# A four-chunk, eight-stage network kernel: the softplus of the Mamba stage split into four planner steps, and a new planned order

## The reference, cut to what matters

```python
u = silu(conv(x_part))                       # 512 columns of a chunk, 128 channels on partitions
delta = jax.nn.softplus(einsum('blr,dr->bld', dt, dt_proj_w) + dt_proj_b)
dA  = jnp.exp(delta * A)                     # A = -exp(A_log), 16 states
dBu = delta * Bm * u
h = dA_t * h + dBu_t                         # scan over time, y = sum over states of h * c_t
```

## Time and profile before

| | before |
|---|---|
| median of 3 runs | 1419.3 us (1419.26 to 1420.51) |
| the profiled execution's own time | 1418.26 us |
| its span in the trace | 1416.4 us |
| TensorE (PE) busy | 1322.8 us, 93% |
| PE weight loads (PEld, beside PE) busy | 923.5 us, 65% |
| VectorE (DVE) busy | 1025.9 us, 72%, 3806 instructions |
| ScalarE (ACT) busy | 896.2 us, 63%, with 78 table loads, 100.1 us |
| GpSimd (POOL) busy | 693.5 us, 49% |
| mean granted TensorE clock | 0.96 of full speed |

### The profile page before, as it was taken

How to read it: one execution, slowest core, us unless ns; L and a number is a source line. 1 busy time by engine, 2 the same in 40 slices (tenths; PEclk the granted TensorE clock), 3 DMA queues, 4 the chain that set the end, 5 groups by cost and what they waited for, 6 DMA issues and landing times. The chain is left out here.

```text
span 1416.4 us, 26262 instructions
## 1 busy us (share of the span) xinstructions
PE 1322.8 (93%) x8774; PEld 923.5 (65%) x8774; DVE 1025.9 (72%) x3806; ACT 896.2 (63%) x2487; POOL 693.5 (49%) x699
## 2 busy tenths in 40 slices
PE   9687698889988999999999999999999999998997
PEld 5123365566545787677777677787777888865665
DVE  4998988787689848668688566497798579653253
ACT  6636689786573558776877776546768657643231
POOL 1637255674374535455445547543825424413625
PEclk9659999999998989999999999999999999999999
DMA  7651000100140100110001000301100000043131
GB/s 266 158 133 30 1 1 2 54 2 29 78 127 1 66 1 3 53 63 1 1 2 61 2 31 31 122 1 61 38 42 2 1 1 2 1 150 102 18 90 30
DMA packets 21278, 65.80 MB, mean 46 GB/s; under 512 B 1852, under 2 KB 8252, under 8 KB 18840
## 3 DMA queue, kind: packets, MB, share of 16 engines
q1 hardware_dynamic: 21144, 64.12, 14.1%
HBM read 61.83 MB, written 2.29 MB: 45 GB/s over the span
## 5 line engine op out<-in xcount | busy, mean ns | idle before, releaser
L1360 ACT ACTIVATE arena<-arena 128x256 f32<-128x256 f32 (+3 forms) x792 | 347.5, 443 | 48.0 <-DVE arena L1828 24.0
L1360 ACT ACTIVATE arena<-bank 128x512 f32<-128x512 f32 (+3 forms) x354 | 190.8, 570 | 237.6 <-PE bank L915 158.1
L915 PE MATMUL bank<-XT,W 128*128 128x512 f32 (+1 forms) x752 | 290.1, 524 | 0.6 <-DVE arena L1828 0.6
L2175 POOL TENSOR_TENSOR arena<-arena 128x256 f32<-128x256 f32 x192 | 119.2, 621 | 331.0 <-DVE arena L1843 330.6
L915 PEld LDWEIGHTS bank<-W,arena 128*128 128x128 f32 (+1 forms) x1888 | 232.2, 195 | 54.1 <-issue 38.0
L915 PE MATMUL bank<-W,arena 128*128 128x128 f32 (+2 forms) x1888 | 244.9, 281 | 7.1 <-POOL arena L2148 4.8
L915 PE MATMUL bank<-arena 128*32 128x128 f32 (+8 forms) x2912 | 238.0, 338 | 11.5 <-DVE arena L1849 3.6
L2148 POOL TENSOR_TENSOR arena<-arena 128x512 f32<-128x512 f32 (+1 forms) x108 | 170.3, 1598 | 121.6 <-DVE arena L1596 74.7
L915 PEld LDWEIGHTS bank<-arena 128*32 128x32 f32 (+4 forms) x2912 | 158.8, 153 | 88.5 <-issue 56.3
L2176 POOL TENSOR_TENSOR arena<-arena 128x512 f32<-128x512 f32 x192 | 203.5, 1060 | 0.0
L915 PE MATMUL bank<-arena,W 128*128 128x512 f32 (+3 forms) x412 | 180.8, 679 | 21.1 <-DVE arena L1755 15.4
(11 more groups left out here) (124 smaller groups left out, 1713.0 us busy)
## 6 DMA issues: line engine op xcount, KB each, us to landing
arena<-rws SPq DMA_DIRECT2D x8, 2048.0 KB, 7.3
arena<-rep SPq DMA_DIRECT2D x62, 256.0 KB, 5.5
arena<-rws SPq DMA_DIRECT2D x4, 1792.0 KB, 6.4
W<-w SPq DMA_DIRECT2D x2, 2124.0 KB, 8.0
arena<-rws SPq DMA_DIRECT2D x8, 384.0 KB, 10.7
W<-w SPq DMA_DIRECT2D x1, 2692.0 KB, 9.7
W<-w SPq DMA_DIRECT2D x1, 2256.5 KB, 8.8
W<-w SPq DMA_DIRECT2D x1, 2002.5 KB, 16.3
```

The costliest lines, as they stand in the source:

```text
L915: return e.matmul(o, lhsT, rhs, start=start, stop=stop, skip_group_check=True)
L1360: return e.activation(o, a, func, **kw)
L2175: e.tensor_tensor(px[:, :, 0:128], px[:, :, 0:128], rec[:, :, 0:1].to_broadcast([128, 2, 128]), ALU.mult)
```

## The change

The step 0.dt becomes four: 0.dt (matmul, four ACT functions, one DVE operation), 0.ln (Ln on ACT, with a table of its own, "n"), 0.dr (three DVE operations: the correction and its sum with relu) and 0.du (two DVE operations, delta and its product with u). What waited for 0.dt now waits for 0.du. The DVE operations are six instead of seven. The fillers are 8 and 3 instead of 10 and 4. Lane 2's tasks have two pairs swapped. All planned lengths (PARTS), the landing times, HASTE, AHEAD and URGENT have new values: URGENT had 98 entries and has some 420; the first table in the planner is now "e".

```diff
-    "0.bc": "P1.78 A.49", "0.wr": "D1.3", "0.rp": "D1.5", "0.da": ("P1.00 A.74", "A.74"), "0.dt": "P1.03 A2.30 V1.66 A.63 V3.22",
-    "0.f": "P.41 A.17", "0.st": "V1.91", "0.db": "G1.27", "0.ac": "P1.50", "0.y": "V.68 P2.88 V.67",
-    "3.h": "P.88 A.63", "3.o": "P3.62 V.69", "4.vz": "G3.00", "4.a": "V.06 P9.59 V.21", "0.b": "P.22 A.16",
-    "4.y": "A.57|V.66", "4.w": "P.89 V.62", "5.r": "P.89 V.54 A.15 V5.88", "5.wt": "P.67 A.56", "5.bb": "P1.04",
+    "0.bc": "P1.77 A.51", "0.wr": "D1.3", "0.rp": "D1.5", "0.da": ("P1.48 A.74", "A.67"),
+    "0.dt": "P1.05 A2.35 V.43", "0.ln": "A.63", "0.dr": "V2.10", "0.du": "V1.40", "0.f": "P.48 A.28", "0.st": "V1.90", "0.db": "G1.27", "0.ac": "P1.50",
+    "3.h": "P.90 A.61", "3.o": "P3.57 V.69", "4.vz": "G1.77", "4.a": "V.09 P12.35 V.21", "0.b": "P.41 A.28",
+    "4.y": "A.57|V.66", "4.w": "P.96 V.69", "5.r": "P.84 V.82 A.21 V4.40", "5.wt": "P.51 A.53", "5.bb": "P1.08",
...
-TABLE = {"0.a": "e", "0.in": "s", "0.dt": "e", "0.da": "e", "0.h": "g", "1.ex": "e", "1.rt": "e", "1.up": "s", "2.t": "e", "3.h": "g",
+TABLE = {"0.a": "e", "0.in": "s", "0.dt": "e", "0.ln": "n", "0.da": "e", "0.h": "g", "1.ex": "e", "1.rt": "e", "1.up": "s", "2.t": "e", "3.h": "g",
...
-        add("0.wr", 0, ("0.dt", 0))
+        add("0.ln", 0, ("0.dt", 0))
+        add("0.dr", 0, ("0.dt", 0))
+        add("0.du", 0, ("0.ln", 0), ("0.dr", 0))
+        add("0.wr", 0, ("0.du", 0))
...
-         [(0, 2), (1, 2), (2, 2), (3, 2), (0, 3), (1, 3), (2, 3), (3, 3), (4, 2), (4, 3), (5, 2), (5, 3),
-          (6, 2), (6, 3), (7, 2), (7, 3)]]
+         [(0, 2), (1, 2), (2, 2), (3, 2), (0, 3), (1, 3), (2, 3), (3, 3), (4, 2), (5, 2), (4, 3), (5, 3),
+          (6, 2), (7, 2), (6, 3), (7, 3)]]
...
 AHEAD = {
-    (0, 0): 773.00, (1, 0): 72.00, (2, 0): -99.00, (3, 0): 1635.00, (4, 0): -846.00, (5, 0): -327.00, (6, 0): -854.00, (7, 0): -3419.00,
-    (0, 1): 802.00, (1, 1): 39.91, (2, 1): -202.00, (3, 1): -293.00, (4, 1): -760.00, (5, 1): -847.00, (6, 1): -785.00, (7, 1): 1712.00,
-    (0, 2): 975.00, (1, 2): 1311.00, (2, 2): 524.00, (3, 2): 1014.00, (4, 2): 1970.00, (5, 2): -554.00, (6, 2): -855.00, (7, 2): 1789.00,
-    (0, 3): 1089.00, (1, 3): -178.00, (2, 3): 1359.00, (3, 3): 1845.00, (4, 3): -450.00, (5, 3): -247.00, (6, 3): -570.00, (7, 3): 828.00,
+    (0, 0): 211.60, (1, 0): 90.23, (2, 0): 91.45, (3, 0): 493.45, (4, 0): 80.13, (5, 0): 249.10, (6, 0): 136.48, (7, 0): 204.34,
+    (0, 1): 9.96, (1, 1): 32.03, (2, 1): 26.73, (3, 1): 420.14, (4, 1): 498.83, (5, 1): 35.15, (6, 1): 49.37, (7, 1): -517.33,
+    (0, 2): 1703.90, (1, 2): 2318.01, (2, 2): 1434.88, (3, 2): 1029.86, (4, 2): 1825.35, (5, 2): 1101.22, (6, 2): 1948.18, (7, 2): 895.16,
+    (0, 3): 1319.81, (1, 3): 1621.24, (2, 3): 449.63, (3, 3): 687.88, (4, 3): 335.99, (5, 3): -80.10, (6, 3): 23.84, (7, 3): 1429.34,
...
-    table = ""
+    table = "e"
...
-                    on.wait_ge(*after("du", "0.dt", c))
+                    on.wait_ge(*after("du", "0.du", c))
...
-            zeros(10)
+            zeros(8)
...
-                        zeros(4)
+                        zeros(3)
...
-                elif name == "0.dt":
-                    on.wait_ge(*after("sf_f", name, c))
-                    on.wait_ge(*after("sf_t", name, c))
+                elif name == "0.ln":
+                    on.wait_ge(*after("sf_f", "0.dt", c))
+                    on.wait_ge(*after("sf_a", "0.dt", c))
+                    on.wait_ge(*after("sf_t", "0.dt", c))
                     act(s0(c, 12), s0(c, 14), ACT.Ln).then_inc(has["sf_n"], 1)
...
-                elif name == "0.dt" and p == 0:
-                    ex, dd = s0(c, 13), s0(c, 15)
-                    on.wait_ge(*after("sf_e", name, c))
-                    ts(s0(c, 14), ex, 1.0, None, ALU.add).then_inc(has["sf_f"], 1)
-                    own(ts(dd, ex, 1.0, -1.0, ALU.add, ALU.add))
-                    on.wait_ge(*own.last())
-                    own(tt(ex, ex, dd, ALU.subtract))
-                elif name == "0.dt":
-                    ex = s0(c, 13)
-                    on.wait_ge(*after("sf_t", name, c))
-                    on.wait_ge(*own.last())
-                    own(stt(ex, s0(c, 4), 1.0, ex, ALU.add, ALU.mult))
-                    on.wait_ge(*after("sf_n", name, c))
-                    on.wait_ge(*own.last())
-                    own(stt(ex, ex, 0.5, s0(c, 12), ALU.mult, ALU.add))
-                    on.wait_ge(*emptied(u("b", name, c)))
-                    on.wait_ge(*own.last())
-                    own(tt(step0(c, 0), ex, s0(c, 11), ALU.add))
+                elif name == "0.dt":
+                    on.wait_ge(*after("sf_e", name, c))
+                    ts(s0(c, 14), s0(c, 13), 1.0, None, ALU.add).then_inc(has["sf_f"], 1)
+                elif name == "0.dr":
+                    ex, dd = s0(c, 13), s0(c, 15)
+                    on.wait_ge(*after("sf_f", "0.dt", c))
+                    own(stt(dd, s0(c, 14), 1.0, ex, ALU.subtract, ALU.subtract))
+                    on.wait_ge(*after("sf_t", "0.dt", c))
+                    on.wait_ge(*own.last())
+                    own(stt(ex, s0(c, 4), 1.0, dd, ALU.add, ALU.mult))
+                    on.wait_ge(*emptied(u("b", "0.dt", c)))
+                    on.wait_ge(*own.last())
+                    own(stt(ex, ex, -0.5, s0(c, 11), ALU.mult, ALU.add))
+                elif name == "0.du":
+                    on.wait_ge(*after("sf_n", "0.ln", c))
+                    on.wait_ge(*own.last())
+                    own(tt(step0(c, 0), s0(c, 13), s0(c, 12), ALU.add))
                     on.wait_ge(*own.last())
                     tt(step0(c, 1), step0(c, 0), s0(c, 6), ALU.mult).then_inc(has["du"], 1)
```

More of the change, by code:

```diff
@@ L151 @@
     "f": {"ve": (0, 1), "rstd": (1, 1), "z": (2, 1)}, "g": {"ve": (0, 1), "rstd": (1, 1), "zg": (2, 1)},
-    "0.w": {"taps": (0, 1)}, "0.dt": {"sf_a": (1, 1), "sf_e": (1, 1), "sf_f": (2, 1), "sf_n": (3, 1), "sf_t": (1, 1), "du": (4, 1)},
+    "0.w": {"taps": (0, 1)}, "0.dt": {"sf_a": (1, 1), "sf_e": (1, 1), "sf_f": (2, 1), "sf_t": (1, 1)}, "0.ln": {"sf_n": (0, 1)}, "0.du": {"du": (0, 1)},
     "0.db": {"dB": (0, 1)}, "0.st": {"hc": (0, 1)},
@@ L239, in stage_steps @@
                 if q == 0:
-                    add(by, 0, ("0.dt", 0))
+                    add(by, 0, ("0.du", 0))
             else:
@@ L245, in stage_steps @@
             else:
-                add("0.da", q, ("0.dt", 0), ("0.a", 0, PREP), *([("0.st", q - 2)] if q >= 2 else []))
+                add("0.da", q, ("0.du", 0), ("0.a", 0, PREP), *([("0.st", q - 2)] if q >= 2 else []))
             if by == "0.rp":
@@ L344 @@
 TASKS = [[(s, 0) for s in range(8)], [(s, 1) for s in range(8)],
-         [(0, 2), (1, 2), (2, 2), (3, 2), (0, 3), (1, 3), (2, 3), (3, 3), (4, 2), (4, 3), (5, 2), (5, 3),
-          (6, 2), (6, 3), (7, 2), (7, 3)]]
+         [(0, 2), (1, 2), (2, 2), (3, 2), (0, 3), (1, 3), (2, 3), (3, 3), (4, 2), (5, 2), (4, 3), (5, 3),
+          (6, 2), (7, 2), (6, 3), (7, 3)]]
 AHEAD = {
[4 rows of a table removed]
-    (0, PREP): -1188.00, (1, PREP): 975.00, (2, PREP): 311.00, (3, PREP): 1229.00, (4, PREP): -248.00, (5, PREP): 2962.00, (6, PREP): -27.00, (7, PREP): -1340.00}
-URGENT = {
[15 rows of a table removed]
[4 rows of a table added]
+    (0, PREP): 1217.35, (1, PREP): -266.05, (2, PREP): 907.74, (3, PREP): -14.66, (4, PREP): 597.99, (5, PREP): 1926.50, (6, PREP): 89.15, (7, PREP): 118.47}
+URGENT = {
[71 rows of a table added]
+    ("g", 2): -34.66, ("g", 3): -46.10, ("load", 0): -48.98, ("load", 1): -76.14, ("load", 2): -72.10}
 HASTE = {
-    "0.b": 1.80, "0.da": 0.04, "0.n": 0.04, "0.wr": 1.60, "1.a": 0.02, "1.rt": 0.20, "3.b": 2.90, "3.o": 0.20, "4.w":
-    1.20, "4.x": 4.10, "5.bb": 1.80, "6.x": 1.10, "7.wt": 0.20}
-LANDS = {("0.n", 2): 3.9, ("0.n", 0): 10.0, ("0.n", 1): 11.3, ("0.w", PREP): 8.6, ("0.a", PREP): 8.6, ("0.f", PREP): 8.6, ("0.b", PREP): 25.0}
+    "0.b": 1.20, "0.n": 0.08, "0.x": 0.17, "1.e": 0.16, "1.wo": 0.05, "1.wt": 0.47, "2.on": 0.04, "2.y": 0.16, "3.x":
+    0.05, "4.b": 0.22, "5.gw": 0.40, "6.a": 1.59, "7.r": 0.17, "7.wt": 0.19, "load": 2.79}
+LANDS = {("0.n", 2): 3.9, ("0.n", 0): 8.9, ("0.n", 1): 10.2, ("0.w", PREP): 8.6, ("0.a", PREP): 8.6, ("0.f", PREP): 9.6, ("0.b", PREP): 25.0}
 OVER = {4: (0,), 5: (1,), 6: (4,), 7: (3, 5)}
```

2 lines of the change are left out of this document (1 added, 1 removed), and 120 rows, old and new, of tables (PARTS, URGENT).

## The result

| | before | after |
|---|---|---|
| median | 1419.28 us (12 runs, 1417.49 to 1423.25) | 1423.08 us (12 runs, 1418.76 to 1427.53) |
| ratio to before | | 1.0023, 95% interval 1.0012 to 1.0034 |
| profiled execution: span | 1416.4 us | 1420.9 us |
| PE busy, idle | 1322.8, 93.6 us | 1321.4, 99.5 us |
| DVE busy | 1025.9 us, 3806 instructions | 1035.4 us, 3804 instructions |

The changed kernel is slower by 0.23%, 3.8 us. The forecast was 1406.

What follows compares the result with a forecast made beforehand. PE was taken as the bound, 1322.8 of 1416.4 us busy, with 77.4 us idle before 496 to win. 1418.3 - 2.2 (softplus) - 11 (order) = 1405.1, with 1.0 for the median 1406 us; range 1391 to 1424.

Steps and rivals of the forecast that it cites:

- the order's term: 142 to 496 us: the newly planned order takes a quarter of PE's 45.6 us idle, -11 us.
- Where the idle time lies, and that PE is the sum: Whole kernel: span is PE busy plus 93.6 us idle, 77.4 of it in the first 496 us.
- The softplus, -2.2 us: Early kernel: -0.5 for fillers, -0.7 for the chain after Ln, -1.0 for less DVE work.
- about three quiet values and one disturbed: Softplus on DVE, four chunks: the removed operation is worth 3 x 0.38 + 1.17 = 2.3, taken as 2 us.
- the bias step: Chunk 2, ahead of Ln on ACT: if the new order moves it, up to 1.7 us more; priced at 0.
- changes no sign: Softplus beside POOL: the scalar_tensor_tensor replacing a tensor_tensor blocks just as long, so the gain keeps its sign.
- The lock of the shared ports: DVE beside POOL: the loser blocks a whole instruction; by this rule the removed operation saves some 5.9 us instead of 2.
- Ln's table: ACT: the planner now knows the two table loads around each Ln, 1.283 us each; counted as 0 on the end.
- Fillers, -0.5 us: PE's start: three instead of four filler matmuls before the first convolution take off about 0.47 us.
- The swapped tasks: Lane 2: two swapped pairs mix an expert stage with attention; 520 to 1275 us has only 4.1 to gain, so 0.
- rival B: Chunk 3's last attention stage runs alone behind an expert stage, PE idles 22 us: 1428; chance 0.17 with other worse orders.
- Rival A: Before 496 us: PE's idle time is really DVE's, so only the softplus counts, 1417; chance 0.12.

Runs made afterwards that it cites:

- e1: Kernel before in its own order, with only the new six-operation softplus on DVE; 1419.49 us, ratio 1.0008.
- e9: Kernel before with POOL's 62 products with B replaced by writes of zeros about as long, reading nothing; 1415.94 us, ratio 0.9969.
- e10: Changed kernel with POOL's products with B replaced by writes of zeros about as long, reading nothing; 1415.90 us, ratio 0.9974.
- e6: Changed kernel with the old AHEAD, URGENT, HASTE and LANDS, and a new order planned from them; 1491.45 us, ratio 1.0511.
- e3: Kernel before with 8 and 3 filler matmuls instead of 10 and 4, nothing else; 1419.14 us, ratio 1.0001.
- e5: Changed kernel with lane 2's old task sequence and a new order planned from it; 1512.37 us, ratio 1.0658.
- e8: Changed kernel with POOL writing one tile of zeros in place of each product with B; 1410.58 us, ratio 0.9942.
- e7: Kernel before with POOL writing one tile of zeros in place of each of its 62 products with B; 1411.42 us, ratio 0.9950.
- e12: Changed kernel, complete, with three waits holding POOL back during the second and third softplus and three products moved; 1412.93 us, ratio 0.9954.
- e11: Kernel before, complete, with three waits holding POOL back during the second and third softplus and three products moved; 1415.42 us, ratio 0.9962.

## Why the prediction was wrong

**The step that failed.** It is the order's term, -11 us: the inference that an order planned from a better list of lengths idles PE less. The idle time in 142 to 496 us went from 45.6 to 49.0 us instead of down to 30 to 38. Of the 17 us between 1406 and 1423, 11 are this gain, 2.2 the gain of the softplus, and 3.8 the loss in place of any gain. The loss is a second failed step: the softplus was priced by the surroundings that it had before, and the new order put it beside POOL's products, where it took 20.8 us instead of 17.7.

**Where the idle time lies, and that PE is the sum**: right. PE busy stayed within 1.4 us, and in the traces the loss is idle time, 5.9 us more.

**The softplus, -2.2 us**: wrong as a sum, and the step that failed is the one that priced the operations by their old surroundings ("about three quiet values and one disturbed") and took the removed one off. The chain did what it should and more: the first write of the products went out at 23.62 us instead of 26.86, 3.24 us where 1.2 were forecast, since the bias step had moved behind Ln as well (its bound of 1.7 us was priced at 0). But POOL's products start with it, at 29.14 instead of 32.11, and run closer. So the second and third softplus fell fully into them. Measured: 20.8 us for 18 operations where some 3 x 3.87 = 11.6 were quiet. That the scalar_tensor_tensor in place of a tensor_tensor "changes no sign" was right for the swap of operations in the old order (e1); the question of where the operations stand beside POOL was never asked.

**The lock of the shared ports**: the Trainium skill (SBUF — State Buffer, "Who interferes with whom") says that a VectorE instruction with two SBUF inputs contends with a GpSimd instruction that reads SBUF and not with one that only writes it. The runs agree: 1.29 us beside products, 0.69 beside writes of the same length. The prediction had the rule in hand and used it as a price for the removed operation, not as a price for the new place of the other six. Its sum by the rule gave each disturbed chunk one block of 1.47 us; at the third softplus the five two-input operations lost 8.20 - 3.5 = 4.7 us, about 0.94 each.

**The order, -11 us**: wrong, and the largest error. Nothing came of it: with POOL's reading away, the orders are equal (e9 and e10), and with POOL held back nearly so (0.9962 and 0.9954, intervals overlapping). What failed is the inference from lengths to the order, "an order chosen by it is wrong locally". The old list was up to 2% off in sum, but its priorities go with it (e6), and the chip runs the old order at its true lengths anyway. Why a new order with priorities of its own gained nothing in 142 to 496 us is argued here and not shown. Two readings behind the term were also off. The waits of the earlier trace rows leave out a third row in 142 to 284 us, 4.0 us of PE waiting for ACT in two pieces, the longer of 3.2, so the waits on other engines than DVE come to 15.3 us and not to 11.3. And the softplus's old 4.88 us was called stale, but the trace of before has 17.7 / 3 = 5.9 us for a chunk, so it was too short and not too long, and the new 3.93 stands against 20.8 / 3 = 6.9 in after. The new list's 2.10 and 1.40 us for 0.dr and 0.du are quiet lengths: they describe the operations alone and are short by 4.7 us at the third softplus. Chunk 2's softplus, with POOL quiet, took 2.29 and 1.42 us for them. So the plan was near the truth where POOL is quiet and wrong at the place where the change put its own steps.

**Ln's table**: the number of table loads in 0 to 142 us fell from 19 to 15, and over the whole it rose from 78 to 83. The term was priced at nothing; no run here separates what the loads cost.

**Fillers, -0.5 us**: the first write came 0.7 us sooner, but nothing of it can be seen at the end (e3).

**The swapped tasks**: 0 was right for the tail as the profile shows it, and rival B didn't come: PE is full in 1311 to 1382 us. By themselves the tasks weren't a separable term at all (e5).

**Rival A** gave 1417 from the softplus alone; its mechanism, that DVE is the bound in the head, was nearest to the truth, but its sign was missing: DVE's work could grow.

The chances had 0.17 on slower, by another mechanism. The time lies inside the stated range, at its upper end, on the wrong side of no change; that it is inside is owed to the room left for rival B, which didn't come.

What stays open: e9 and e10 are equal in time but not in its parts. In 0 to 496 us PE idles 67.4 us in e9 (24.9 + 21.1 + 21.4) and 79.8 in e10 (29.5 + 26.8 + 23.5), while over the whole span PE is busy for 1329.1 us in e9 and 1318.6 in e10, at a mean granted clock of 0.954 and 0.959. The sign is the same in every pair: over the whole span the new order idles PE 5.9 us more in after than in before, 4.4 in e8 than in e7, 10.7 in e10 than in e9, 5.6 in e12 than in e11. So the idle time that the new order adds in the traces doesn't go with the contention, though the difference in time does. These are single profiled executions, and no run separates whether the new order itself leaves PE more idle and the clock gives it back, or whether both move with something else.

## What to carry to other kernels

A planned length holds only beside the neighbours it was measured with: a DVE operation with two SBUF inputs costs 0.69 us alone and 1.3 to 1.7 beside a POOL operation that reads SBUF, so plan such pairs apart, or let the engine with slack wait (three waits on POOL, with three products moved, gave 0.4% to the kernel before and 0.7% to the changed one). Judge a re-planned order by the idle time of the bound engine in each stretch and by the time of many executions, since the two can disagree (e9 and e10), and don't mix priorities, lengths and tasks of different plans: one part taken back alone cost 5 to 7%. When work is moved earlier, ask which other engine starts earlier with it, and what it then meets.
